# A transformer block pair on one core: first layer norm moved into the recurrence, stores awaited later, last tiles reordered

## Chip, cores, metric

One core of a Trainium2 chip. The metric is the device time of one launch in microseconds (us), the median of several runs. Engines are named as in the profile: PE is TensorE, DVE is VectorE, ACT is ScalarE, POOL is GpSimd, SP is SyncE, which issues all DMAs of this kernel.

## What is computed

Two blocks of the same outer form over x of 4 batches, 512 positions and 512 channels, in fp32. Of the reference only the outer form and the second block matter here:

```python
xn = layernorm(x)
x = x + attention0(xn) * silu(ffn0(xn))          # a recurrence over time, and a gated FFN
xn = layernorm(x)                                # of x1, as the kernel names it
# attention1: linear attention, 16 heads of 128, keys and values of 4 heads
q, k, v = xn @ Wq.T + bq, xn @ Wk.T + bk, xn @ Wv.T + bv
sq, sk = elu(q) + 1, elu(k) + 1
kv = einsum('bhsd,bhse->bhde', sk, v)
s = (sq @ kv) / (sum over d of sq * k_sum + 1e-6) @ Wo.T
# ffn1: relu between two products, weights of 4 bits with scales, plus a rank of 16
g = silu(relu(xn @ W_up + b_up + xn @ A_up @ B_up) @ W_dn + b_dn + relu(...) @ A_dn @ B_dn)
x = x + s * g
```

## The kernel before

Four stages follow each other, each a block of its own with a barrier of all engines at its end: `front` (norm and projections of attention 0), `recurrence_and_gate`, `linear_attention`, `relu_gate`. A batch is a tile of 128 partitions by 4 rows of 512 (TT = 4 tiles of 128 positions; KT = 4 tiles of 128 channels). The order of work is written out by hand for every engine; engines meet by semaphores. Products in full precision are made of three matmuls on split operands (`product3`, L701 to L703): a high part (rounded copy) and a low part (the rest). Buffers `relay[0..2]` (1 MB each) and `parts` outlive the stages and carry data over a barrier: loads for the next stage are issued before the barrier and counted by `handed`/`hand`.

`recurrence_and_gate`: VectorE's `unit` and GpSimd's `read` run the recurrence, TensorE the FFN. In the end of the last batch (`finish`, `silu`, then `attend` for t = 0 to 3) VectorE gates the attention's tiles, GpSimd's `add` adds them to x into `xs`, and SyncE stores each tile of x1 (L967) and waits until all have landed. Before that SyncE loads x1 of batch 0 into `relay[0]`, Wk into `relay[1]`, Wv into `relay[2]`.

`linear_attention`: the first batch needs `statistics`, `deviations` (GpSimd, a power), `normalise`, then TensorE's transposes (L2043), ScalarE's high parts `copy_x` (L1937), VectorE's low parts `low_x` (L1789). Beside it `high_kv` (L1928) and `low_kv` (L1702) split Wk and Wv. Then come products k and v of each batch, kv, and for 64 pairs of head and batch q, M and the heads; `accumulate` (L1852) sums the heads into `acc[b]`. At the end SyncE stores s of each batch and tile (L1691, 16 stores) and waits for all.

`relu_gate`: 16 steps a batch (UT = 16). Step j makes the up product of tile j; ReLU on ScalarE (L2425), the split of x2 on VectorE (L2377, L2379), and two steps later (LAG = 2) the down products for t = 0 to 3. In the first batch the weights of 4 bits are expanded beside it, two tiles a step: `expand` on VectorE (L2330, L2334), with a small product by `make` (L2452), `high` on ScalarE (L2397), the low part on GpSimd (L2297). A `make` of tile i waits for the expansion of tile i - 2. In the last steps the results of a batch are finished: z, tanh, gate on VectorE and ScalarE, and GpSimd adds to x1 in `xs` (two tiles), which SyncE loads and stores tile by tile.

## Time and profile before

| | |
|---|---|
| median of 3 runs | 1770.9 us (1768.85 to 1771.44) |
| profiled execution | 1772.48 us, its span 1770.7 us, mean granted clock 0.968 |
| PE busy | 1641.4 us (93%), 6704 matmuls |
| DVE busy | 1177.9 us (67%) |
| ACT busy | 394.4 us (22%) |
| POOL busy | 615.4 us (35%) |
| DMA | 200.45 MB, mean 113 GB/s |

```profile
PE   6899947999999999969999999999996899999996
DVE  6999755777878778746637777787875566242423
PEclk9999977999999999989999999999999899999998
DMA  5534457675676765513020000000003433101011
```

The four strips show the span in 40 equal slices of 44.3 us, each digit the busy share in tenths; PEclk is the granted clock of TensorE in tenths of full speed (2.4 GHz; 5 is 1.2 GHz). The recurrence ends in slice 18, the linear attention in slice 31, and `relu_gate` fills the rest. A busy PE is not PE at its peak: the ends of matmuls are modelled.

### The profile page before, as it was taken

To read this page: it belongs to the slowest core of one execution; us is meant where nothing else is said; L and a number is where in the kernel's file an instruction comes from. 1 tells how busy PE (TensorE), PEld (TensorE's weight loads), DVE (VectorE), ACT (ScalarE), POOL (GpSimd) and SP (SyncE) were. 2 spreads that over 40 slices of the span, in tenths; PEclk is the share of its full clock that TensorE was granted. 3 is DMA by queue.
4 is the path that set the end of the run, shared out by engine and by line. 5 is a ranking of instruction groups with operands and counts; after the bars stand their busy time and mean duration, and the time that the engine had idled before them with its cause. 6 is when DMAs were issued, how large, how long until landed. Compare 5 with 4: busy or idle time off the path is not lost. (4 is left out here: it accounts for less than half of the span.)

```text
span 1770.7 us, 20395 instructions
## 1 busy us (share of the span) xinstructions
PE 1641.4 (93%) x6704; PEld 1135.9 (64%) x6704; DVE 1177.9 (67%) x1694; ACT 394.4 (22%) x670; POOL 615.4 (35%) x455
## 2 busy tenths in 40 slices
PE   6899947999999999969999999999996899999996
PEld 3344425647646656528877777777774667888885
DVE  6999755777878778746637777787875566242423
ACT  1222220011021110112223333333332222121211
POOL 4586522445554565450003222232421242010101
PEclk9999977999999999989999999999999899999998
DMA  5534457675676765513020000000003433101011
GB/s 196 194 123 170 180 173 238 227 213 200 202 224 206 232 200 196 179 39 116 24 91 29 18 24 14 25 18 19 19 3 141 126 104 101 64 30 65 30 41 36
DMA packets 87329, 200.45 MB, mean 113 GB/s; under 512 B 7248, under 2 KB 29520, under 8 KB 79440
## 3 DMA queue, kind: packets, MB, share of 16 engines
q1 hardware_dynamic: 87248, 199.42, 33.9%
q8 instruction: 44, 0.72, 0.2%
q14 instruction: 37, 0.30, 0.1%
HBM read 156.41 MB, written 42.99 MB: 113 GB/s over the span
## 5 line engine op out<-in xcount | busy, mean ns | idle before, releaser
L986 POOL TENSOR_TENSOR r_rS<-r_S,r_rT 128x512 f32<-128x512 f32 x128 | 184.6, 1444 | 206.2 <-DVE r_S L1079 204.0
L1852 DVE SCALAR_TENSOR_TENSOR l_acc<-l_ps,l_inv,l_acc 128x512 f32<-128x512 f32 x240 | 167.3, 749 | 10.1 <-PE l_ps L703 10.1
L1079 DVE TENSOR_TENSOR_SCAN r_S<-r_dT,r_ps 128x512 f32<-128x512 f32 x128 | 156.4, 1222 | 17.3 <-POOL r_rS L986 13.2
L2377 DVE CAST g_x_part<-g_x 128x512 fp32r<-128x512 f32 x64 | 36.8, 574 | 188.6 <-ACT g_x L2425 188.6
L1430 PE MATMUL r_ps<-Wdn,r_h 128*128 128x512 f32 x352 | 154.6, 595 | 0.0
L1725 POOL TENSOR_TENSOR relay<-l_expq,l_reluq 128x512 f32<-128x512 f32 x42 | 54.4, 1295 | 190.7 <-ACT l_expq L2004 190.7
L1430 PEld LDWEIGHTS r_ps<-Wdn,r_h 128*128 128x128 f32 x352 | 65.7, 190 | 85.5 <-issue 85.4
L2304 POOL TENSOR_TENSOR g_xs<-g_xs,relay 128x512 f32<-128x512 f32 x16 | 21.4, 1336 | 262.3 <-DVE relay L2355 250.8
L1828 DVE TENSOR_SCALAR l_expq<-l_ps,l_bq 128x512 f32<-128x512 f32 x64 | 48.0, 750 | 89.0 <-ACT l_reluq L2000 86.9
L701 PE MATMUL l_ps<-l_M_part,l_sq_part 128*128 128x512 f32 x256 | 101.6, 397 | 3.9 <-DVE l_acc L1852 3.1
L701 PE MATMUL g_ps<-g_Wdn,g_x_part 128*128 128x512 f32 x256 | 103.7, 405 | 0.0
L701 PE MATMUL r_ps<-relay_part,r_w_part 128*128 128x512 f32 x224 | 94.4, 422 | 10.0 <-DVE r_h L1090 7.2
L702 PE MATMUL g_ps<-g_Wdn,g_x_part 128*128 128x512 f32 x256 | 101.2, 395 | 0.0
L703 PE MATMUL g_ps<-g_Wdn,g_x_part 128*128 128x512 f32 x256 | 101.2, 395 | 0.0
L703 PE MATMUL l_ps<-l_M_part,l_sq_part 128*128 128x512 f32 x256 | 100.7, 393 | 0.0
L702 PE MATMUL l_ps<-l_M_part,l_sq_part 128*128 128x512 f32 x256 | 100.3, 392 | 0.0
L703 PE MATMUL r_ps<-relay_part,r_w_part 128*128 128x512 f32 x224 | 91.2, 407 | 0.0
L702 PE MATMUL r_ps<-relay_part,r_w_part 128*128 128x512 f32 x224 | 91.1, 407 | 0.0
L2425 ACT ACTIVATE g_x<-g_ps,g_b_up 128x512 f32<-128x512 f32 x64 | 43.8, 685 | 205.7 <-PE g_ps L703 205.7
L2000 ACT ACTIVATE l_reluq<-l_ps,l_bq 128x512 f32<-128x512 f32 x64 | 44.1, 689 | 199.2 <-PE l_ps L703 199.1
L1285 ACT ACTIVATE r_tanh_gate<-r_ps 128x512 f32<-128x512 f32 x44 | 26.3, 597 | 274.7 <-PE r_ps L703 274.7
L701 PE MATMUL r_ps<-relay_part,first_part 128*128 128x512 f32 x128 | 55.4, 433 | 26.8 <-DVE relay_part L1059 22.4
(278 smaller groups left out, 3921.2 us busy)
## 6 DMA issues: line engine op xcount, KB each, us to landing
r_w_part<-scratch_wgu SPq DMA_DIRECT2D x28, 1024.0 KB, 7.0
r_V<-scratch_v SPq DMA_DIRECT2D x96, 256.0 KB
first_part<-scratch_wgu SPq DMA_DIRECT2D x16, 1024.0 KB, 5.4
relay<-scratch_x SPq DMA_DIRECT2D x11, 1024.0 KB, 6.7
scratch_wgu<-f_halves SPq DMA_DIRECT2D x28, 384.0 KB, 4.4
relay<-scratch_v SPq DMA_DIRECT2D x32, 256.0 KB
relay<-in_x SPq DMA_DIRECT2D x4, 1024.0 KB, 8.2
scratch_x<-f_xT SPq DMA_DIRECT2D x4, 1024.0 KB
```

The source lines that it names most:

```text
L701: nc.tensor.matmul(out, left[1], right[0], start=start, stop=False)
L702: nc.tensor.matmul(out, left[0], right[1], start=False, stop=False)
L703: return nc.tensor.matmul(out, left[0], right[0], start=False, stop=stop)
L986: nc.gpsimd.tensor_tensor(rS[u % RS][:, :], S[u % 2][:, 0:T], rT[u // DK][:, :], ALU.mult).then_inc(rS_ready.sem, 1)
L1079: nc.vector.tensor_tensor_scan(S[u % 2][:, 1:T + 1], dT[hh][:, :], kv, 0.0, ALU.mult, ALU.add).then_inc(S_ready.sem, 1)
L1430: last = nc.tensor.matmul(place[0][:, :], h[:, j, n * P:(n + 1) * P], Wdn[:, j, :], start=(j == 0), stop=(j == JT - 1))
L1725: nc.gpsimd.tensor_tensor(sq[i % N_SQ], expq[i % 2][:, :], reluq[i % 2][:, :], ALU.add).then_inc(sq_ready, 1)
L1828: nc.vector.tensor_scalar(expq[i % 2][:, :], place("q", i)[:, :], bq[:, h:h + 1], 0.0, ALU.add, ALU.min).then_inc(minq_ready, 1)
L1852: last = nc.vector.scalar_tensor_tensor(acc[b][:, t, :], ps, scale, acc[b][:, t, :], ALU.mult, ALU.add)
L2000: nc.scalar.activation(reluq[i % 2][:, :], place("q", i)[:, :], ACT.Relu, bias=bq[:, h:h + 1]).then_inc(reluq_ready, 1)
L2377: nc.vector.tensor_copy(hi[:, :], x2[j % 2][:, :]).then_inc(x2_hi_ready.sem, 1)
L2425: nc.scalar.activation(x2[j % 2][:, :], U.place(("up", j))[:, :], ACT.Relu, bias=b_up[:, j:j + 1]).then_inc(x2_ready.sem, 1)
```

## The change

In the recurrence's end VectorE makes the whole layer norm of batch 0 (`next_normalised`) between the last `silu` and the `attend`s, with the power on GpSimd, in place in `relay[0]`. The last of the four additions of x1 goes from GpSimd to VectorE. The stores of x1's last batch count on `x1_late`, which the stage doesn't await; the linear attention awaits it on SyncE before the load of batch 3 and on VectorE before the key operations. There the statistics and the normalisation of batch 0 are gone, the low parts 0 and 1 of Wk are made by VectorE, and ScalarE copies x between the splits of Wk and Wv.

At the end of the linear attention s goes out in four stores, one a batch, counted on `s_late` and awaited by SyncE in `relu_gate` ahead of the first load of s. There ScalarE's first ReLU waits for b_up alone, and in step 0 ReLU and split come before the expansions. The last batch of TensorE is written out behind the loop; its last 12 down products run tiles 0 and 1 first, then tile 2, then tile 3 (`END`). x1 is loaded whole into `relay[1]` (4 tiles), and the words of W_dn have a buffer of their own.

```diff
@@ recurrence_and_gate, SyncE
             sp.wait_ge(*F.product(("gu", JT - 1), B - 1))
-            sp.dma_start(relay[0][:, :, :], rows(x1, 0)).then_inc(hand, 16)
+            sp.dma_start(relay[0][:, :, :], rows(x1, 0)).then_inc(next_x_loaded, 16)
...
             for t in range(TT):
-                sp.wait_ge(*x1_ready.now(B, t + 1))
-                sp.dma_start(x1[(B - 1) * T + t * P:(B - 1) * T + (t + 1) * P, :], xs[:, t, :]).then_inc(
-                    x1_stored.sem, 16)
-            sp.wait_ge(x1_stored.sem, 16 * (B + TT))
+                if t < TT - 1:
+                    sp.wait_ge(*x1_ready.now(B, t + 1))
+                else:
+                    sp.wait_ge(last_x1_ready, 1)
+                sp.dma_start(x1[(B - 1) * T + t * P:(B - 1) * T + (t + 1) * P, :], xs[:, t, :]).then_inc(x1_late, 16)
+            sp.wait_ge(x1_stored.sem, 16 * B)
@@ GpSimd
             body(B - 1, False, True)
-            for t in range(TT):
+            pool.wait_ge(next_step, 3)
+            nc.gpsimd.tensor_tensor(next_rstd[:, :], next_veps[:, :], half[:, 0:TT], ALU.pow).then_inc(next_step, 1)
+            for t in range(TT - 1):
                 add(B, t)
@@ VectorE
+            def next_normalised():
+                dve.wait_ge(next_x_loaded, 16)
+                for t in range(TT):
+                    last = nc.vector.bn_stats(next_stats[:, t, :], relay[0][:, t, :])
+                last.then_inc(next_step, 1)
...
+                for t in range(TT):
+                    last = nc.vector.bn_aggr(next_mv[:, t, :], next_stats[:, t, :])
+                last.then_inc(next_step, 1)
+                dve.wait_ge(next_step, 2)
+                nc.vector.tensor_scalar(next_veps[:, :], next_mv[:, :, 1], 1e-5, None, ALU.add).then_inc(next_step, 1)
+                dve.wait_ge(next_step, 4)
+                for t in range(TT):
+                    nc.vector.tensor_scalar(relay[0][:, t, :], relay[0][:, t, :], next_mv[:, t, 0:1], next_rstd[:, t:t + 1],
+                                            ALU.subtract, ALU.mult)
...
                 silu(b, 3)
+                next_normalised()
                 for t in range(TT):
                     attend(b + 1, t, F.place(("s", 0)) if t < 2 else O)
+                dve.wait_ge(*x_loaded.before(b + 1, 1))
+                dve.wait_ge(*sg_ready.now(b + 1, TT))
+                nc.vector.tensor_tensor(xs[:, TT - 1, :], xs[:, TT - 1, :], u1[TT - 1], ALU.add).then_inc(last_x1_ready, 1)
@@ linear_attention, SyncE
-            sp.wait_ge(handed, 3 * 16)
...
             sp.wait_ge(*product("xT", 1, KT - 1))
+            sp.wait_ge(x1_late, TT * 16)
             load_x(3)
...
             for b in range(B):
-                for t in range(TT):
-                    sp.wait_ge(acc_ready, ((QH - 1) * B + b) * TT + t + 1)
-                    sp.dma_start(slab(spill["s"], b)[:, t * C:(t + 1) * C], acc[b][:, t, :]).then_inc(s_stored, 16)
-            sp.wait_ge(s_stored, 16 * B * TT)
+                sp.wait_ge(acc_ready, ((QH - 1) * B + b + 1) * TT)
+                sp.dma_start(slab(spill["s"], b), flat(acc[b][:, :, :])).then_inc(s_late, 16)
@@ GpSimd
-            low_kv("k", 0)
-            low_kv("k", 1)
-            deviations(0)
+            pool.sem_inc(rstd_ready, 1)
             low_kv("k", 2)
             low_kv("k", 3)
@@ VectorE
-            statistics(0)
-            normalise(0)
+            for s in (stats_ready, mv_ready, var_ready):
+                dve.sem_inc(s, 1)
+            dve.sem_inc(xn_ready, TT)
+            for kt in range(2):
+                dve.wait_ge(wkv_hi_ready["k"], kt + 1)
+                nc.vector.tensor_tensor(Wkv["k"][1][:, kt, :], raw["k"][:, kt, :], Wkv["k"][0][:, kt, :].bitcast(F32),
+                                        ALU.subtract).then_inc(wkv_lo_ready["k"], 1)
             low_x(0)
+            dve.wait_ge(x1_late, TT * 16)
@@ ScalarE
-            act.wait_ge(handed, 3 * 16)
+            act.wait_ge(handed, 2 * 16)
             high_kv("k")
+            copy_x(0)
             high_kv("v")
-            copy_x(0)
@@ relu_gate
+    END = [(t, i) for i in range(UT - 1 - LAG, UT) for t in range(2)]
+    END += [(t, i) for t in range(2, TT) for i in range(UT - 1 - LAG, UT)]
...
-        xs = sb("xs", [P, 2, C])
-        up_q, dn_q = s[:, :, :].bitcast(I32), xs[:, :, :].bitcast(I32)
+        xs = relay[1]
+        dn_words = sb("dn_words", [P, 2, C], I32)
@@ SyncE
-                load(0)
-                load(1)
+                sp.wait_ge(*out_stored.before(b, TT))
+                sp.dma_start(xs[:, :, :], rows(x1, b)).then_inc(x1_loaded.sem, 16)
                 for t in range(TT):
                     sp.wait_ge(*out_ready.now(b, t + 1))
-                    sp.dma_start(out[bass.ds(b * T + t * P, P), :], xs[:, t % 2, :]).then_inc(out_stored[t % 2].sem, 16)
-                    if t + 2 < TT:
-                        load(t + 2)
+                    sp.dma_start(out[bass.ds(b * T + t * P, P), :], xs[:, t, :]).then_inc(out_stored.sem, 16)
...
             sp.wait_ge(expanded, 2 * len(order))
+            sp.wait_ge(s_late, 16 * B)
             finish(0)
@@ VectorE (ScalarE likewise with high(x))
-                    if first:
+                    if first and j > 0:
                         for x in tiles_at(j):
                             expand(x)
...
                     nc.vector.tensor_tensor(lo[:, :], x2[j % 2][:, :], hi[:, :].bitcast(F32), ALU.subtract).then_inc(
                         x2_lo_ready.sem, 1)
+                    if first and j == 0:
+                        for x in tiles_at(j):
+                            expand(x)
@@ ScalarE
-                    act.wait_ge(small_loaded, 2 * 16)
+                    act.wait_ge(b_up_loaded, 16)
@@ TensorE
+                    if last_batch and n == UT - 1:
+                        for t, i in END:
+                            pe.wait_ge(*x2_lo_ready.now(b, i + 1))
+                            product = down(b, t, i)
+                            if i == UT - 1:
+                                product.then_inc(Y.done.sem, 1)
+                        return
...
-            with pe.Fori(1, B) as b:
+            with pe.Fori(1, B - 1) as b:
                 sequence(b, False)
+            sequence(B - 1, False, True)
```

## Rows read from the trace of the kernel before

**Rows 1.** Stretches: us, busy (instructions) of each engine, PEclk, DMA share, GB/s.
```profile
800.50:930.00 129.50, 128.53 (x674) 104.77 (x672) 68.52 (x128) 33.48 (x64) 8.77 (x8) 1.00 0.22 73
1373.60:1402.34 28.74, 25.56 (x81) 17.32 (x81) 16.16 (x22) 6.88 (x12) 9.36 (x8) 0.81 0.42 114
...
1430.90:1459.86 28.96, 27.47 (x104) 18.79 (x105) 17.37 (x24) 7.43 (x13) 10.44 (x9) 1.00 0.37 109
...
1500.00:1757.00 257.00, 256.36 (x1110) 208.10 (x1108) 80.82 (x131) 41.02 (x63) 12.84 (x10) 1.00 0.12 42
```
**Rows 2.** Order of time, PE: start, us, line, out<-in, count [idle before <-releaser].
```profile
793.64 0.45 PE L2043 MATMUL l_ps<-ident,relay 128*128 128x128 f32 x1 [11.89 <-DVE relay L1783]
...
800.45 0.53 PE L701 MATMUL l_ps<-l_Wk,kept_x_part 128*128 128x512 f32 x1
```
**Rows 3.** Chain that ended last, start of the stage relu_gate: start, us, what.
```profile
1373.22 0.34 SPq L2255
...
1378.24 5.18 DMA g_b_dn<-in_b_dn
```
**Rows 4.** The same chain, at the end of the span.
```profile
1754.47 0.70 DVE kept_scale L2347
...
1766.92 1.28 POOLq L2130
```
**Rows 5.** Line L967, SyncE's stores of x1: ns min/median/max of the issue.
```profile
L967 SPq DMA_DIRECT2D scratch_x<-r_xs x4: 332/338/349, 780.5 to 785.1; - x4
...
DMA to landing us min/median/max: 2.0/2.0/2.0
```
**Rows 6.** Order of time, DVE, from the recurrence's end on.
```profile
778.36 1.41 DVE L1165 SCALAR_TENSOR_TENSOR r_u<-r_ps,r_hyr,r_u 128x512 f32<-128x512 f32 x2 [5.76 <-PE r_ps L1358]
781.79 1.41 DVE L1165 SCALAR_TENSOR_TENSOR r_u<-r_ps,r_hyr,r_u 128x512 f32<-128x512 f32 x2 [2.02 <-PE r_ps L1358]
787.59 2.47 DVE L1769 BATCH_NORM_STATS2 l_stats<-relay 128x6 f32<-128x512 f32 x4 [4.39 <-PEq L753]
...
792.02 5.69 DVE L1783 TENSOR_SCALAR relay<-relay,l_mv,l_rstd 128x512 f32<-128x512 f32 x4 [1.14 <-POOL l_rstd L1707]
...
818.37 1.92 DVE L1783 TENSOR_SCALAR relay<-relay,l_mv,l_rstd 128x512 f32<-128x512 f32 x4 [1.13 <-POOL l_rstd L1707]
```
**Rows 7.** Order of time, ACT (first row) and POOL.
```profile
787.58 2.19 ACT L1928 ACTIVATE l_Wk<-relay 128x512 fp32r<-128x512 f32 x4 [14.73 <-PEq L753]
...
782.62 2.48 POOL L999 TENSOR_TENSOR r_xs<-r_xs,r_u 128x512 f32<-128x512 f32 x2 [0.88 <-DVE r_u L1165]
...
788.36 2.50 POOL L1702 TENSOR_TENSOR l_Wk<-relay,l_Wk 128x512 fp32r<-128x512 f32 x2 [0.64 <-ACT l_Wk L1928]
```
**Rows 8.** Stretches of one us at the stage's start, for PEclk (third from the end).
```profile
787.00:788.00 1.00, 0.00 (x0) 0.00 (x0) 0.41 (x1) 0.42 (x1) 0.16 (x2) 0.50 0.00 0
...
800.00:801.00 1.00, 1.00 (x6) 0.96 (x5) 0.84 (x2) 0.80 (x2) 0.07 (x1) 0.72 0.07 16
```
**Rows 9.** Line L1691, SyncE's stores of s: ns min/median/max of the issue.
```profile
L1691 SPq DMA_DIRECT2D scratch_s<-l_acc x16: 424/709/1062, 1355.6 to 1367.0; - x16
...
DMA to landing us min/median/max: 5.4/6.5/6.9
```
**Rows 10.** Stretches for DMA: the last two columns are its share and GB/s.
```profile
1360.00:1365.00 5.00, 1.87 (x9) 1.21 (x7) 2.66 (x4) 0.00 (x0) 0.00 (x0) 1.00 1.05 396
...
1375.00:1380.00 5.00, 5.00 (x17) 3.55 (x17) 1.04 (x2) 0.00 (x0) 0.00 (x0) 0.76 0.78 229
```
**Rows 11.** Order of time in the expansion, DVE (first row) and PE.
```profile
1387.34 0.68 DVE L2330 SCALAR_TENSOR_TENSOR g_whole<-relay,g_z 128x512 f32<-128x512 int32 x1
...
1385.22 0.80 PE L701 MATMUL g_ps<-kept_x_part,kept_up 128*128 128x512 f32 x1 [1.92 <-ACT g_x L2425]
1385.81 0.63 PE L702 MATMUL g_ps<-kept_x_part,kept_up 128*128 128x512 f32 x1
1386.24 0.63 PE L703 MATMUL g_ps<-kept_x_part,kept_up 128*128 128x512 f32 x1
```
**Rows 12.** Order of time, DVE, its last instruction.
```profile
1763.15 0.69 DVE L2355 SCALAR_TENSOR_TENSOR relay<-relay,g_z 128x512 f32<-128x512 f32 x1
```

More of the change, by code:

```diff
@@ L1457, in _, with linear_attention @@
                 counted = F.index[job] + 1
-def linear_attention(nc, w, x1, spill, relay, parts, ident, kept, handed, hand):
+def linear_attention(nc, w, x1, spill, relay, parts, ident, kept, handed, x1_late, hand, s_late):
     UNITS = QH * B
@@ L2107, in _, with relu_gate @@
                 last.then_inc(done, 1)
-def relu_gate(nc, w, x1, spill, out, relay, parts, kept, handed):
+def relu_gate(nc, w, x1, spill, out, relay, parts, kept, handed, s_late):
     LAG = 2
@@ L2426, in sequence @@
                                          bias=b_up[:, j:j + 1]).then_inc(x2_ready.sem, 1)
+                    if first and j == 0:
+                        for x in tiles_at(j):
+                            high(x)
             act.sem_inc(w_hi_ready, len(first_tiles))
@@ L2591, in build, with stages @@
         handed = [outer.enter_context(nc.semaphore(f"handed{i}")) for i in range(3)]
-        stages(nc, w, out, spill, x1, relay, parts, ident, handed)
-def stages(nc, w, out, spill, x1, relay, parts, ident, handed):
+        x1_late = outer.enter_context(nc.semaphore("x1_late"))
+        s_late = outer.enter_context(nc.semaphore("s_late"))
+        stages(nc, w, out, spill, x1, relay, parts, ident, handed, x1_late, s_late)
+def stages(nc, w, out, spill, x1, relay, parts, ident, handed, x1_late, s_late):
     with ExitStack() as ctx:
@@ L2614, in stages @@
         kept["narrow"] = sb("narrow", [P, C])
[L2615 to L2616 removed]
+        linear_attention(nc, w, x1, spill, relay, parts, ident, kept, handed[1], x1_late, handed[2], s_late)
+        relu_gate(nc, w, x1, spill, out, relay, parts, kept, handed[2], s_late)
 def kernel(**inputs):
```

65 lines of the change are left out of this document (33 added, 32 removed).

## The prediction

> **What bounds the kernel now.** I read the stages first (busy time by stretch), then the waits and the order of time at the three places where the stretches leave holes. [rows 1]: in the first 129.5 us of the linear attention TensorE is busy 128.5 us, and in the last 257 us before the end 256.4 us. These stretches are bound by TensorE: what is won ahead of them arrives at the end whole. In the expansion of the weights (from 1373.6) it is busy 25.6 of 28.7 us at a mean clock of 0.81, later 27.5 of 29.0: there the expansion by VectorE, ScalarE and GpSimd leads, and TensorE has about 1.5 us of slack in each 29. Three holes remain.
> Hole A: TensorE is done with the recurrence at 781.8, starts its transposes at 793.64 after 11.89 us idle, and the first key product at 800.45 [rows 2].
> Hole B: the last accumulation ends at 1362.66, and SyncE's first instruction of the next stage is at 1373.22 [rows 3]. The expansion then starts slowly.
> Hole C: the last product ends about 1756.4, the span at 1770.7 [rows 4].
>
> **Part A, norm and stores.** Before: the last store of x1 is issued at 785.1 and lands 2.0 us later [rows 5], and the end barrier comes after it; then statistics, GpSimd's power and normalisation (787.59 to 797.71), transposes, copies.
> The norm is moved into VectorE's idle time of 5.76 us ahead of 778.36 [rows 6]. Its price there: from the start of the statistics to the power's result 4.43 us (787.59 to 792.02), and four normalisations at 0.48 us as in the row of 818.37, where GpSimd rests, not 1.42 us as at 792.02, where it works [rows 6]. That is 4.43 + 1.92 = 6.35 us, 0.6 us more than the gap. The first two gatings slip by that; the last two wait for a product that ends at 781.8 and don't move. So the norm costs nothing on the path (bounds: 0, and 0.6 if all slips). Its power is queued on GpSimd behind the last inverse and ahead of the additions; GpSimd is idle there. Its load of relay[0] is far ahead.
> The last addition goes from GpSimd (ends 785.10 [rows 7]) to VectorE, behind the last gating at 783.20. VectorE takes 0.69 us for such an operation alone; beside GpSimd's third addition (to about 783.9) it waits at most for that one. I take 784.5. SyncE issues the last store in 0.35 us and no longer waits for its landing; the barrier took 0.4 us after the landing. New start of the stage: 785.4 instead of 787.55, won 2.15 us (bounds 1.6 and 2.7). Three small loads queue on SyncE behind the stores; their reader comes 6 us later.
> In the new stage ScalarE splits Wk first (2.19 us for four [rows 7]), then copies x, then splits Wv. Low parts 0 and 1 of Wk are VectorE's, 2 and 3 GpSimd's: the third high part is there at 1.7 us, two GpSimd operations of 1.25 us [rows 7] end at 4.2. Beside it, transposes 0.3 to 4.0 even at the low clock, copies from 2.2 on, VectorE's low x from 2.9 to 5.7. TensorE's key product starts at 4.4 us of the stage instead of 12.9 (800.45 less 787.55), 8.5 us sooner. GpSimd has the low parts of Wv at about 10.8, their use is at about 16. The wait for x1_late stands on VectorE ahead of the key operations, at about 6 us of the stage; the stores (2 us) have long landed. On SyncE it stands before the load of batch 3.
> TensorE's clock: the granted clock was at 0.50 from 787 and rose within 800 to 801 [rows 8], after 2.7 us of dense transposes; so the old products started nearly at 2.4 GHz. Now only some 2 us of transposes stand ahead of them, behind 4 us of rest. If 3 us of products lie at 1.2 GHz, half is lost, 1.5 us; bounds 0 and 1.7. I take 1.5, since the nearest stretch, the transposes from 793.64 to 800, lay wholly at the low level. Sum A: 2.15 + 8.5 - 1.5 = **9.1 us** (7.3 to 11.2). Behind it TensorE is the bound [rows 1], so it stays.
> VectorE's two low parts of Wk have two operands in SBUF, and GpSimd works beside the second. [rows 6] show 1.42 against 0.48 us with and without GpSimd. The Trainium skill (GPSIMD Engine Reference, Specifications) says that the SBUF interfaces are shared with VectorE, in two-port modes or with two SBUF inputs. By that the second low part would wait for one GpSimd operation, and the low x would start some 0.3 us later. The sum can do without it.
>
> **Part B, s and the expansion.** Before: 16 stores of 256 KB, issued from 1355.6 to 1367.0 at 709 ns each, landing 5.4 to 6.9 us after issue [rows 9], and SyncE waits for the last. I read that as a backlog: the DMA engines are full at 396 GB/s in 1360 to 1365 [rows 10].
> Now: four stores of 1 MB, the last issued at 1362.7, not awaited. Issue 0.4 to 0.6 us, barrier 0.5: start of the stage about 1363.8 instead of 1373.22, 9.4 us sooner. But the 5.24 MB (s, and 1 MB of up_q issued at 1355.05) are not fewer: at 400 GB/s from about 1356.9 they end at 1370.0. All loads of the new stage are queued behind: b_up lands at about 1370.5 instead of 2.2 us after issue; up_scale, dn_q and the first dn_scale are 1.0 MB, 3.5 us at the 290 GB/s that this mix would give (229 at a share of 0.78 [rows 10]), so dn_scale lands at 1374.3.
> This rests on order in the queue, for which the landing times grown to 6.9 us speak. The Trainium skill (DMA: Bandwidth & Descriptors, Queues, rings and completion order) says that on each engine descriptors are consumed in ring order; by that, the trace agrees, small loads don't overtake the stores, which speaks against part of this change's gain.
> Then: the first product needs 5.1 us at 1.2 GHz (twelve matmuls 0.43 us apart, as 1385.81 and 1386.24 [rows 11]) and is done at about 1369.5. ScalarE waits only for b_up, so its first ReLU (before: after two weight splits that waited for b_dn, which landed at 1383.42 [rows 3]) is at 1370.6. VectorE splits x2 to 1372.6, expands its first tile to 1374.0, the second 1374.3 to 1375.7 (its scale); GpSimd's low part of the first ends at 1376.0, so the third tile starts at 1376.1. Before it started at 1387.34 [rows 11]: **11.2 us** sooner. From there the same instructions follow in the same order, with the same loads of up_q.
> TensorE: its third up product waits for the second tile's expansion, because a small product is queued ahead of it: 1376.2, against 1385.22 [rows 11], 9.0 us sooner and, as before, at the low clock. It is 2.2 us behind the expansion's gain, and has slack of 1.5 us in each stretch: used up by the second, so the 11.2 stay. Bounds: 6.6 (below, SyncE held) and 14.
> The bigger SBUF buffers and the split semaphore for b_dn cost nothing: b_dn is first used in the next batch.
>
> **Part C, end.** TensorE does the same last 12 products in another order, tiles 0 and 1 first; x2's last part is there at 1750.0 and now used at 1750.6, so it doesn't stall. Tile 0 is done 4 products earlier, 12 matmuls of 0.234 us, 2.8 us, tile 3 as before. VectorE's end chain starts at 1751.7 instead of 1754.47 and, with z of tile 3 at 1757.2 (product at 1756.4), ends at 1761.2 instead of 1763.84 [rows 12]. GpSimd's last addition no longer waits for a store and a load into the same buffer (the addition started at 1766.92 [rows 4]): it runs 1761.2 to 1762.5, and 2.5 us for the last store, as before, end at 1765.0. Won **5.7 us**. If the other order helped nothing, 3.1; bounds 3.1 and 6.0. x1 whole (1 MB) and s are loaded some 70 us earlier; SyncE loses its waits between them. The last batch written out behind the loop costs code to fetch; the loop's turns before show no gap [rows 1]. Bounds 0 and 1 us, I take 0.
>
> **Sum.** 9.1 + 11.2 + 5.7 = 26.0 us. The profiled execution took 1772.5 us (span 1770.7); it would take 1746.5. It lies 1.6 above the median of 1770.9, so the median would be **1744.9**.
>
> **Rivals.**
> (1) The forecast as above, 1741 to 1748: chance 0.50.
> (2) No backlog for the new loads, and the clock up sooner in A: B gives 13 to 14 (then TensorE's own work binds), A 10.5: about 1741, down to 1738. For it: 8 KB of b_up could pass; against it: the stores' landing times. By the Trainium skill's rule of ring order this case doesn't come. 0.17.
> (3) SyncE is held: 709 ns an issue against 338 for stores of x1 [rows 5, 9] says that it is throttled when much is queued. Four stores of 1 MB may block it until the queue has room, in the worst case to 1370. Then the first product ends at 1375.1, ReLU, split and two tiles take 5.6 us, the third tile starts at 1380.7, B gives 6.6 and the total is 21.4: 1749.5. 0.23.
> (4) A or B yields still less (later loads of weights, low clock in both, 17 to 20 us won): 1751 to 1754. 0.06.
> (5) Slower than before: TensorE stays at 1.2 GHz through much of the expansion, because its products come in shorter pieces between the new waits. Each us of product there costs 0.5 us. To eat 26 us, some 52 us of the 86 must lie at the low level beyond today's 11; from 60 us on the kernel is slower by over 0.2%. All 75 more would cost 37 and give 1782. Against it: in the stretch from 1430.9 it stood at 1.00 with the same rhythm [rows 1]. 0.02.
> (6) It does not do what it says: SyncE's end of the stage still comes only when all stores have drained, in A and in B, and the loads come behind it: little more than C is left, near 1762 to 1767. 0.02.
>
> **How the numbers follow.** The likeliest case gives 1744.9. For 8 in 10 the range takes in (1), (2) and (3) nearly whole: 1738 to 1752. What a measurement of this kernel can tell is about 0.2%, 3.5 us. Faster by more 0.96, within 0.02, slower 0.02.
>
> **What would show it.** A: no VectorE statistics at the stage's start, last gating still near 783.2, key product 4.4 us behind the first load of biases; if 6 or more, Wk's low parts are late. The clock row of the first 4 us of products tells 1.5 from 0. B: the issue of the last store of s near 1362.7; if next-stage loads are issued after 1367, it is (3); the landing time of b_up, 6 us or 2, tells (1) from (2); third tile's start relative to 1376.1 (shifted by A). C: span's end 8.6 us behind the last product instead of 14.3. It would be wrong if TensorE, at the low clock, were the last thing in the expansion's stretches.

## The result, and the profile after

| | before | changed |
|---|---|---|
| first timing, median | 1771.17 us (4 runs) | 1755.53 us (1749.87 to 1757.08, 4 runs) |
| ratio, 95% interval | | 0.9905 (0.9882 to 0.9928) |
| second timing, ratio | | 0.9884 (0.986 to 0.9909) |
| third timing, ratio | | 0.9886 (0.9862 to 0.9911) |
| profiled execution, span | 1772.48, 1770.7 us | 1749.87, 1748.1 us |

The change won 15.6 us by the first timing; the mean of the three ratios is 0.9892, or 19.1 us. The forecast was 26.0 us and 1744.9: the direction was right, the size too large, and the 1755.5 lies above the upper end of the range, 1752.

PE, DVE and the granted clock of the changed kernel in 40 slices of its span:

```profile
PE   6899846899999999989999999999998899999997
DVE  6999855777877879756637777787777466242423
PEclk9999977999999999999999999999999899999999
```

The strips are nearly those of before: the gain lies in three places that are shorter than a slice of 44 us. So I compare landmarks instead, instructions that every variant has. The work before the first landmark, the start of the last s-projection of the recurrence, ends anywhere from 770.3 to 775.0 in 17 profiles, whichever the kernel: that is scatter and belongs to no part.

| profile | s-proj. to first key product | to last accumulation | to last product | to end of span | third tile |
|---|---|---|---|---|---|
| before | 27.50 | 562.21 | 393.70 | 14.34 | 24.7 |
| changed | 16.35 | 563.71 | 387.01 | 9.46 | 18.2 |
| changed, second profile | 16.69 | 565.55 | 385.99 | 9.49 | 17.7 |
| changed, third profile | 16.34 | 563.80 | 388.54 | 9.49 | 19.0 |

Each column is the time from the landmark to its left, in us; the last one is the start of the third expanded tile behind the last accumulation (before: 1387.34 [rows 11] less 1362.66). The first column is A, the second the clock's share of it, the third B, the fourth C. The s-projection takes 7.1 us in some profiles and 8.8 in others, with part of it at 1.2 GHz, so A has to be read between profiles alike in that: without A the first two columns sum to 588.0 to 588.2 (three profiles, 7.1) and 589.7 (before, 8.8); with A to 580.1 (four) and 581.9 to 582.2 (four). Run 11 below, also without A, has 592.6: the same code lost 2.9 us more to the low clock there. The means of all profiles, 589.3 in the five without A and 581.1 in the eight with A and no fillers, differ by 8.2. **A is worth 7.6 to 8.2 us by the profiles.** B's column is 392.3 to 393.7 in the four profiles without B, mean 393.1, and 386.0 to 388.5 in the five that have all three parts with B's code as the change has it, mean 387.3: **B is worth 5.8 us** (3.8 to 7.7 between single profiles; 5.6 if run 3, B alone at 388.8, is counted in). **C is worth 4.85.** Together 18.4 to 18.9, beside 19.1 by the timings.

What B did is seen in SyncE's rows of the changed kernel and in the last accumulation's (start, us, engine, line):

```profile
1348.84 2.79 DVE L1877 SCALAR_TENSOR_TENSOR l_acc<-l_ps,l_inv,l_acc 128x512 f32<-128x512 f32 x4 [1.07 <-PE l_ps L703]
...
1344.05 0.55 SPq L1718 DMA_DIRECT2D relay<-in_up_q  x1
1344.65 7.34 SPq L1722 DMA_DIRECT2D scratch_s<-l_acc  x4
1352.66 0.34 SPq L2282 DMA_DIRECT2D g_b_up<-in_b_up  x1
```

The last accumulation ends at 1351.63, and the stage's first load is issued 1.03 us behind it; before it was 10.56 (1362.66 to 1373.22 in [rows 3]). The views of these two lines (ns min/median/max of the issue, then time to landing):

```profile
L1722 SPq DMA_DIRECT2D scratch_s<-l_acc x4: 332/378/611, 1344.6 to 1351.7; - x4
DMA to landing us min/median/max: 9.0/10.2/11.8
...
DMA to landing us min/median/max: 8.9/8.9/8.9
```

A store of s is issued in 378 ns instead of 709 [rows 9]: SyncE is not held. But a store of 1 MB lands after 10.2 us, and the 8 KB of b_up, the last line, after 8.9. Why, the stretches of the changed kernel show (last two columns: share and GB/s of the DMA engines):

```profile
1345.00:1350.00 5.00, 3.51 (x16) 2.61 (x15) 3.93 (x7) 0.00 (x0) 0.00 (x0) 1.00 0.89 227
1350.00:1355.00 5.00, 2.61 (x10) 1.85 (x9) 1.63 (x3) 0.00 (x0) 0.00 (x0) 0.91 1.02 428
1355.00:1360.00 5.00, 5.00 (x17) 3.46 (x17) 0.00 (x0) 0.00 (x0) 0.00 (x0) 0.75 1.00 411
1360.00:1365.00 5.00, 1.22 (x6) 0.66 (x4) 1.12 (x2) 0.69 (x1) 0.00 (x0) 0.93 1.03 229
```

The stores go at 411 to 428 GB/s, as reckoned. The load of up_q ahead of them moves only 227 GB/s at a share of 0.89, the first packets of the stores included, and the loads of scales and of the first words of W_dn behind them 229 at 1.03. ScalarE and VectorE wait for what stands at the end of that queue:

```profile
1361.54 0.69 ACT L2454 ACTIVATE g_x<-g_ps,g_b_up 128x512 f32<-128x512 f32 x1 [18.28 <-DMA g_b_up<-in_b_up]
...
1366.09 0.69 DVE L2356 SCALAR_TENSOR_TENSOR g_whole<-relay,g_z 128x512 f32<-128x512 int32 x1 [2.67 <-DMA g_z<-in_up_scale]
...
1367.93 0.69 DVE L2356 SCALAR_TENSOR_TENSOR g_whole<-g_dn_words,g_tanh_z 128x512 f32<-128x512 int32 x1 [0.43 <-DMA g_tanh_z<-in_dn_scale]
...
1369.88 0.69 DVE L2356 SCALAR_TENSOR_TENSOR g_whole<-relay,g_z 128x512 f32<-128x512 int32 x1 [0.54 <-POOL g_Wup L2324]
```

These are the first ReLU and the expansions of the first three tiles: 9.9, 14.5, 16.3 and 18.2 us behind the last accumulation. The forecast had 7.9, 9.9, 11.6 and 13.4.

### The profile page after: what moved, and what is told of

It reads as the page before. It is cut to its first block and busy times, and to the rows that moved or that the text cites. A ratio compares the mean times of both kernels' runs of the same rounds, so it can differ in the third digit from the quotient of the medians.

```text
span 1748.1 us, 20338 instructions
## 1 busy us (share of the span) xinstructions
PE 1635.2 (94%) x6704; PEld 1132.9 (65%) x6704; DVE 1179.0 (67%) x1697; ACT 394.1 (23%) x670; POOL 612.9 (35%) x452
## 5 line engine op out<-in xcount | busy, mean ns | idle before, releaser
L2331 POOL TENSOR_TENSOR relay<-relay 128x512 f32<-128x512 f32 x16 | 21.7, 1355 | 257.1 <-DVE relay L2381 257.1
L701 PE MATMUL r_ps<-relay_part,r_w_part 128*128 128x512 f32 x224 | 92.9, 415 | 10.9 <-DVE r_h L1102 8.1
L702 PE MATMUL r_ps<-relay_part,r_w_part 128*128 128x512 f32 x224 | 89.6, 400 | 0.0
L703 PE MATMUL r_ps<-relay_part,r_w_part 128*128 128x512 f32 x224 | 89.5, 400 | 0.0
```

What stands on the lines that cost most here:

```text
L701: nc.tensor.matmul(out, left[1], right[0], start=start, stop=False)
L702: nc.tensor.matmul(out, left[0], right[1], start=False, stop=False)
L703: return nc.tensor.matmul(out, left[0], right[0], start=False, stop=stop)
```

## The experiments

All timings stand beside runs of the kernel before on the same chip: runs 1 to 4 together, then 5 to 8, 9 to 12, 13 to 15. "Third tile", "last product" and the like are counted behind the last accumulation, as in the table above.

**Run 1, the changed kernel again.**

> The changed kernel as it is, timed beside its parts. The theory (backlog in B, and a clock that falls or not at short waits of TensorE): 14 to 22 us won over the kernel before, with single runs 5 us or more apart, since its four runs lay between 1749.9 and 1757.1. In the trace, counted from the end of the last accumulation: the third expanded tile starts 18.3 us later. The rival (the first trace was a lucky run, the loss lies in a stage that was not looked at): some stretch other than the stage starts differs from the first trace by more than 3 us.

Measured: 1752.06 us, ratio 0.9884 (0.986 to 0.9909), span 1750.5; its landmarks stand above. The third tile starts at 17.7 (expected 18.3), and the gain is nearer to 20 us than to the first timing's 15.6.

**Runs 2 to 4, each part alone** (the other parts' lines as in the kernel before):

```diff
@@ A alone: norm in the recurrence, x1_late
+                next_normalised()
@@ B alone: unawaited stores, early ReLU
+                sp.dma_start(slab(spill["s"], b), flat(acc[b][:, :, :])).then_inc(s_late, 16)
@@ C alone: order of the end, x1 whole
+                        for t, i in END:
+                sp.dma_start(xs[:, :, :], rows(x1, b)).then_inc(x1_loaded.sem, 16)
```

> Part A alone (norm of the first batch in the recurrence's end, stores of x1 not awaited, Wk's low parts shared, x copied ahead of Wv). Theory from the two traces: 11.1 us won, less a dip of the clock in the linear attention now and then (1.5 us): 9.5 to 11. My blind sum had 9.1. Rival: A wins its 11 us at its own place, but less arrives at the end (under 7), because the linear attention or the expansion gives it back.

Measured: 1761.97, ratio 0.9937 (0.9914 to 0.996). s-projection to last accumulation 582.06 (before 589.71), the rest as before. That is 7.65 us, while the ratio of the timing says 11 (7 to 15); the profile is of one of the slower executions of run 2. So theory and rival, 9.5 to 11 us or under 7, are not clearly told apart; 7.65 lies between them.

> Part B alone (s in four stores not awaited, ReLU ahead of the expansion in step 0, b_up on its own semaphore). Theory: 6 to 7 us won, since the loads of the stage come behind the stores of s: from the last accumulation to the third tile 18 to 18.5 us instead of 24.7. The blind sum had 11.2. Rival: B is worth 11 alone and only the combination with A loses.

Measured: 1766.9, ratio 0.9968 (0.9952 to 0.9985). Last accumulation to last product 388.84 instead of 393.1, third tile at 18.0. B falls short alone too, so the rival is out. The landmarks give 4.3 us, less than the expected 6 to 7, which the timing (5.7, 2.7 to 8.5) leaves open.

> Part C alone (last products in another order, x1 whole in a buffer of four tiles). Theory: the span's end 9.4 us behind the last product instead of 14.3, 4.9 us won; blind 5.7. Rival: the batch written out behind the loop, or the 1 MB load, costs in the last batches: under 3 us won, and the stretch between the expansion's end and the last product is longer than before's 296.5 us.

Measured: 1766.49, ratio 0.9976 (0.9957 to 0.9994). Last product to end 9.47 instead of 14.34, the other columns as before: the expected 4.9 us.

The three parts stand in three separate columns, with 7.65, 4.3 and 4.9 us alone: 16.9, against 18.4 in the whole, within the scatter of B's column. So nothing shows that the forecast's gain was lost between the parts; by the landmarks each was sized too large by itself, B most.

**Run 5, a quarter of s stored.** This kernel leaves out three quarters of s, in the stores and in the later loads.

```diff
-                sp.dma_start(slab(spill["s"], b), flat(acc[b][:, :, :])).then_inc(s_late, 16)
+                sp.dma_start(slab(spill["s"], b)[:, 0:C], acc[b][:, 0, :]).then_inc(s_late, 16)
...
-                sp.dma_start(flat(s[:, :, :]), slab(spill["s"], b)).then_inc(s_loaded.sem, 16)
+                sp.dma_start(s[:, 0, :], slab(spill["s"], b)[:, 0:C]).then_inc(s_loaded.sem, 16)
```

> The changed kernel, but each of the four stores of s writes only its first quarter (256 KB of 1 MB), and the load of s in the last stage reads only that quarter; three quarters of s are left out. Theory 1 (backlog): the loads of the next stage were late only because 4 MB of stores lay ahead of them. Then b_up lands 2 to 4 us behind its issue instead of 8.9, up_scale before the first ReLU is through, and the third expanded tile starts at most 14 us behind the last accumulation instead of 18.2: 4 to 6 us sooner than in the changed kernel, some 5 us less in the whole. Theory 2 (the loads are slow by themselves: broadcast scales, bytes of up_q): b_up lands sooner, the scales do not, and the third tile starts 17 to 18 us behind, within 1 us of the changed kernel. Theory 3 (the gain is eaten by TensorE's clock in the expansion): the third tile starts sooner, but the tile behind the next load of up_q stays 41 to 43 us behind the last accumulation.

Measured: 1745.69 us, ratio 0.9846 (0.9828 to 0.9863). b_up lands after 2.6 us, and the first ReLU waits for TensorE and no longer for a DMA:

```profile
1357.08 0.69 ACT L2454 ACTIVATE g_x<-g_ps,g_b_up 128x512 f32<-128x512 f32 x1 [14.65 <-PE g_ps L703]
```

It is 6.3 us behind the last accumulation, the third tile 12.8, the last product 383.3. Theory 1 holds: the bytes of the stores account for 4.0 us (387.3 less 383.3) of the 5.4 that B lacked. The step from there to the last product takes 370.5 us, against 369.0 before and 368.8 in the changed kernel, so 1.5 to 1.8 us are left for theory 3.

**Run 6, the stores issued by ScalarE's queue.**

```diff
+                act.wait_ge(acc_ready, ((QH - 1) * B + b + 1) * TT)
+                act.dma_start(slab(spill["s"], b), flat(acc[b][:, :, :])).then_inc(s_late, 16)
@@ relu_gate, ScalarE, ahead of the first expanded tile's high part
+                    act.wait_ge(s_late, 16 * B)
```

> The changed kernel, but the four stores of s are issued by ScalarE's queue at the end of its program instead of SyncE's; ScalarE waits for their landing ahead of the high part of the first expanded tile. Theory 1 (order within a queue): the next stage's loads on SyncE's queue do not stand behind the stores any more; they only share the engines' bandwidth with them. b_up lands in 3 to 5 us instead of 8.9, and the third tile starts 14 to 16 us behind the last accumulation instead of 18.2: 2 to 4 us less in the whole than the changed kernel. Theory 2 (the bytes are the limit, not the order): 5 MB must go through anyway, the scales land as late as before, and the time stays within 1 us of the changed kernel's. ScalarE's wait could cost up to 1 us if the stores land later than 13 us behind the last accumulation.

Measured: 1750.11, ratio 0.9878 (0.986 to 0.9896). The scales come sooner, the first tile starts at 10.9 us instead of 14.5, the third at 15.6 instead of 18.2, as theory 1 had it; but the last product is at 385.9, the time of theory 2, beside 386.0 to 388.5 in the changed kernel. No store stands ahead of b_up in its queue any more, and still it lands 8.0 us after issue, against 8.9. What does stand ahead of it there is the load of up_q. Time to landing of up_q (first line) and b_up:

```profile
DMA to landing us min/median/max: 12.6/12.6/12.6
...
DMA to landing us min/median/max: 8.0/8.0/8.0
```

The load of up_q took 12.6 us here and 7.1 in the changed kernel. It was issued at 1342.84 and landed at 1355.4, 3.9 us behind the issue of b_up; b_up landed at 1359.5, just behind the last store (1359.3). What held up_q, the DMA queues show from 1346 to 1354 (q10 is ScalarE's, q1 SyncE's; packets, MB, share of the 16 DMA engines):

```profile
q10 hardware_dynamic: 358, 2.67, 79.0%
q1 hardware_dynamic: 361, 0.74, 23.9%
```

The two queues took turns packet by packet, and a store's packet held 8 KB where one of up_q held 2 KB. The Trainium skill (DMA: Bandwidth & Descriptors, Queues, rings and completion order) says that an engine serves its queues in turn, packet by packet; the trace agrees. So the order in the queue, the forecast's reason, held b_up behind up_q, and the stores held both from another queue, by their turns. How a small load fares with nothing ahead of it in its own queue was not tried.

**Run 7, TensorE kept busy in two pauses of the linear attention.** The fillers are products whose results are overwritten.

```diff
+FILL_K, FILL_Q = 7, 8
...
+                            for _ in range(FILL_K):
+                                nc.tensor.transpose(out[:, 0:P], ident[:, :], ident[:, :])
                         pe.wait_ge(wkv_lo_ready[kind], KT)
@@ ahead of the first product with the second head's Wq
+                                for _ in range(FILL_Q):
+                                    nc.tensor.matmul(out[:, :], x_part[b][0][:, 0, 0:P], x_part[b][0][:, 0, :],
+                                                     start=True, stop=True)
```

> The changed kernel, with two fillers on TensorE in the linear attention, whose results are overwritten: seven 128x128 transposes of the identity between the transposes of batch 0 and the first key product, and eight 128x512 products ahead of the first product with the second head's Wq, where TensorE waited 2.1 us. Theory 1 (the clock takes part of A): without the pauses the granted clock stays or rises, the first key products are 0.23 us apart instead of 0.43, and the dip behind the 2.1 us wait goes; from first key product to last accumulation 562.5 us as in the kernel before, instead of 563.7 to 565.5; 1 to 3 us less in the whole. Theory 2 (the clock does not hang on these pauses): the stretch stays at 563.7 to 565.5, and the fillers cost up to 0.5 us.

Measured: 1750.75, ratio 0.9875 (0.9858 to 0.9891). First key product to last accumulation 562.29: theory 1. The gain of 1.4 to 3.3 us in this stretch is clear in the traces and too small for these timings.

**Run 8, the changed kernel without the early ReLU.**

```diff
-                    if first and j > 0:
+                    if first:
                         for x in tiles_at(j):
                             expand(x)
```

> The changed kernel with one edit of part B undone: the first ReLU and split again follow the expansion of the first two tiles, and ScalarE waits for b_up and b_dn together. The forecast counted on the early ReLU and split (they were to run while the scales are awaited). Theory 1 (scales late, backlog): the first tile waits for up_scale to about 14 us behind the last accumulation whatever the order is, so moving ReLU and split behind the tiles puts 2 to 3 us of work back on the path: the third tile starts 20 to 21 us behind instead of 18.2, and the whole takes 1.5 to 3 us more. Theory 2 (the order does nothing, all of B is the stores): within 0.5 us of the changed kernel.

Measured: 1758.04, ratio 0.9914 (0.9896 to 0.9933). Third tile at 21.2, last product at 389.7: 2.4 us behind the mean of the changed kernel. Theory 1: while the scales are awaited, ReLU and split are free.

**Run 9, two stores ahead of up_q.** SyncE waited for the load of up_q until 1344.05, while the first two sums had been ready at 1338.3 and 1342.7 and the DMA engines rested.

```diff
+            for b in range(2):
+                sp.wait_ge(acc_ready, ((QH - 1) * B + b + 1) * TT)
+                sp.dma_start(slab(spill["s"], b), flat(acc[b][:, :, :])).then_inc(s_late, 16)
             sp.wait_ge(*sq_split(UNITS - 1))
             sp.wait_ge(*product("rows", QH - 1))
             sp.dma_start(relay[0][:, :, :].bitcast(I32),
...
-            for b in range(B):
+            for b in range(2, B):
```

> The changed kernel, with the stores of s of batches 0 and 1 issued ahead of the load of up_q that SyncE issues last but one in the linear attention. Their sums are ready at 1338.3 and 1342.7 in the changed kernel's trace, but SyncE stood until 1344.05 at the wait for that load and issued all of them behind it; the DMA engines rested before. Theory 1 (backlog of bytes): 2 MB are gone by then, b_up lands 3 to 6 us behind its issue instead of 8.9, the third tile starts 13 to 15.5 us behind the last accumulation instead of 18.2, and the whole takes 2 to 4 us less than the changed kernel, nearly as little as with a quarter of s stored. Theory 2 (what delays the loads is not bytes but the broadcast scale loads, or TensorE's clock eats the gain): the third tile starts sooner, the whole takes within 1 us of the changed kernel's time.

Measured: 1749.9, ratio 0.9862 (0.9842 to 0.9881). Stores and b_up of this kernel, time to landing, in this order: the first two stores, the last two, b_up.

```profile
DMA to landing us min/median/max: 3.9/4.0/4.2
...
DMA to landing us min/median/max: 4.4/5.4/6.4
...
DMA to landing us min/median/max: 3.6/3.6/3.6
```

Third tile at 12.6, last product at 381.5, where the forecast had thought the changed kernel (393.7 less 11.2). All of s is stored. Theory 1.

**Run 10, the stores of run 9, the two fillers of run 7, and nine more fillers at the attention's end.** Beside run 9, the last of these:

```diff
+            pe.wait_ge(*reader[jobs[len(jobs) - len(banks)]])
+            for _ in range(FILL_END):
+                nc.tensor.matmul(banks[len(jobs) % len(banks)][:, :], x_part[0][0][:, 0, 0:P], x_part[0][0][:, 0, :],
+                                 start=True, stop=True)
```

> The kernel with the stores before up_q, and with three fillers on TensorE, whose results are overwritten: the two of the run before (ahead of the first key product, and ahead of the first product with the second head's Wq), and nine 128x512 products behind the last product of the linear attention, in the 2.4 us in which TensorE waits for the next stage. Theory 1 (the clock hangs on the pauses): from the end of the s-projection to the last accumulation 570.3 us as in the run with the two fillers (573.0 in the changed kernel), and the first product of the last stage takes 2.8 us instead of 4.6 from first to last matmul, which counts if b_up has landed by then; 3 to 5 us less in the whole than the stores before up_q alone. Theory 2 (the two gains overlap: the last stage is held by the loads, not by the product): only the 2.7 us of the two fillers.

Measured: 1746.78, ratio 0.9842 (0.9826 to 0.9859). s-projection to last accumulation 579.2; last product at 383.5. The first product of the last stage is through sooner, but b_up was issued 1.8 us behind the last accumulation instead of 1.0, and the first tile waits 1.09 us for its scale. Theory 2 on the last stage: what held it was the loads, not the first product.

**Run 11, the order of the end alone.** Of part C only `END`; x1 in quarters as before.

```diff
+                        for t, i in END:
+                            pe.wait_ge(*x2_lo_ready.now(b, i + 1))
+                            product = down(b, t, i)
```

> The kernel before with one half of part C: in the last batch the products with Wdn go in the new order, tiles 0 and 1 first; x1 is still loaded in quarters into two buffers. Theory 1 (the forecast's split: 2.6 us from the order, 3.1 us from the whole load of x1): the span ends 11.7 us behind the last product instead of 14.3. Theory 2 (the halves overlap: with tiles 0 and 1 done sooner, their stores and the loads into their buffers are done sooner as well, so GpSimd's last addition does not wait any more): it ends 9.5 to 10 us behind, as with both halves, and the whole load of x1 is worth nothing here.

Measured: ratio 0.9991 (0.9978 to 1.0003), span 1771.4. The timing can't tell it from the kernel before. This profile's attention lost 2.9 us more to the low clock (565.1 us from first key product to last accumulation, against 562.2), which hides in the span what the end won. Its code there is that of the kernel before, and still the clock was low at the first key products and fell behind the wait of 2.1 us (products 0.43 us apart, as at 1.2 GHz):

```profile
935.39 0.77 PE L701 MATMUL l_ps<-kept_x_part,l_Wq_part 128*128 128x512 f32 x1 [2.10 <-POOL l_Wq_part L1711]
935.95 0.63 PE L702 MATMUL l_ps<-kept_x_part,l_Wq_part 128*128 128x512 f32 x1
936.38 0.63 PE L703 MATMUL l_ps<-kept_x_part,l_Wq_part 128*128 128x512 f32 x1
```

Last product to end 11.5 us instead of 14.3: theory 1. The order is worth 2.8 us (forecast 2.6), the whole load 2.0 (forecast 3.1). Why the second half fell short, VectorE's last row shows here (first) and in the changed kernel:

```profile
1763.90 0.69 DVE L2356 SCALAR_TENSOR_TENSOR relay<-relay,g_z 128x512 f32<-128x512 f32 x1
```

```profile
1742.66 1.63 DVE L2381 SCALAR_TENSOR_TENSOR relay<-relay,g_z 128x512 f32<-128x512 f32 x1
...
1742.10 1.64 POOL L2331 TENSOR_TENSOR relay<-relay 128x512 f32<-128x512 f32 x1 [1.35 <-DVE relay L2381]
```

With x1 there in whole, GpSimd's third addition runs beside VectorE's last gate, and both take longer: 1.63 instead of 0.69. That gate ends at 1744.29, 0.55 us behind the addition, which had started first. In run 11 a load holds GpSimd's third addition until 1764.23, when that gate is half through; there the gate takes 0.69 and the addition 1.49 us instead of 1.26. Before it was 0.69 as well [rows 12]. The Trainium skill (GPSIMD Engine Reference, Specifications) says that the two engines share SBUF interfaces, with contention for VectorE's instructions of two SBUF inputs; this trace agrees.

**Run 12, the stores of s alone** (the stores and their late wait, the first step in its old order).

```diff
+                sp.wait_ge(acc_ready, ((QH - 1) * B + b + 1) * TT)
+                sp.dma_start(slab(spill["s"], b), flat(acc[b][:, :, :])).then_inc(s_late, 16)
```

> The kernel before with one half of part B: four stores of s that the stage does not wait for; first ReLU and split behind the first two tiles as before, b_up and b_dn awaited together. Theory 1 (the halves add up, as the changed kernel without the early ReLU says): the first load of the last stage 1.0 us behind the last accumulation instead of 10.6, the third tile 21.2 us behind it instead of 24.7, last product 389.7 to 390.5 us behind it instead of 393.7, so 3.2 to 4 us less in the whole. Theory 2 (the stores alone are worth nothing, since ScalarE waits for b_dn at the end of a backlog): the third tile 23.5 us behind or later, under 1.5 us in the whole.

Measured: 1771.34, ratio 0.9986 (0.9972 to 1.0001). Third tile at 21.6, last product at 390.6, 2.5 us less than without B: nearer to theory 1, just past its weak end. So 9.4 us at the stage's start became 2.5 at its end.

**Runs 13 to 15.** The changed kernel; the stores of run 9 with the two fillers of run 7; the changed kernel with the first filler alone.

> The changed kernel unaltered, beside the two below. By the traces' sum (A 7.5 to 8.0, B 6.7 to 7.7, C 4.9) it takes 19 to 20.6 us less than the kernel before, a ratio of 0.989; if the first timing was right and the traces flatter it, 0.9905 or more.

> The stores of s of batches 0 and 1 before the load of up_q, and the two fillers of the linear attention, without the nine at its end. Theory 1 (the gains add: 573.3 to 570.3 us from the s-projection to the last accumulation by the fillers, 386.5 to 381.5 from there to the last product by the stores; the end fillers cost 2 us, since SyncE's first load came 0.75 us later and the scales with it): 7 to 8 us less than the changed kernel, 1.5 to 2 less than with the end fillers as well. Theory 2 (the 381.5 of that one profile was chance of the clock): 383 to 384 again, 5 to 6 us less than the changed kernel.

> The changed kernel with the seven transposes ahead of the first key product alone. Theory 1 (two losses of about 1.5 us each, one at the first products, one behind the 2.1 us wait at 919): from first key product to last accumulation 563.7 us instead of 565.5 (both) and 562.3 (none), and the dip behind the wait stays. Theory 2 (the dip is an echo of the low clock at the start): with the first products at full clock the dip is gone too, 562.3.

Measured: 1753.42, 1746.66 and 1754.53 us; ratios 0.9886 (0.9862 to 0.9911), 0.9854 (0.983 to 0.9879) and 0.9896 (0.9869 to 0.9922).

| run | key product to last accumulation | to last product | third tile |
|---|---|---|---|
| 13 | 563.80 | 388.54 | 19.0 |
| 14 | 562.28 | 384.27 | 13.3 |
| 15 | 562.42 | 387.39 | 18.4 |

Run 13's ratio is the expected 0.989, but its B column gives 4.6 us, not the expected 6.7 to 7.7. Run 14 is 6.8 us faster than run 13 beside it by the medians (the intervals of the ratios overlap a little), and 7.0 in the spans; with run 10 it is the second kernel that lies well below the changed one, at 1746.7 and 1746.8 us. Its second theory was the right one on the last stage: the 381.5 of run 9 did not come again. The three kernels with the stores ahead have 381.5, 384.3 and 383.5, mean 383.1, so that edit is worth 4.2 us beyond the change; the end fillers do nothing that can be told.

In run 15, with the first filler alone, both losses of clock are gone, though the wait of 2.1 us stays (one profile). Rows of TensorE's granted clock (third from the end) behind that wait, in the second profile of the changed kernel and in run 15:

```profile
920.00:925.00 5.00, 2.90 (x10) 1.97 (x9) 3.28 (x3) 1.93 (x4) 3.77 (x3) 0.80 0.32 102
925.00:930.00 5.00, 5.00 (x23) 3.15 (x22) 0.75 (x1) 1.75 (x4) 0.35 (x1) 0.86 0.02 4
```

```profile
920.00:925.00 5.00, 4.28 (x23) 2.90 (x23) 3.18 (x4) 1.32 (x2) 1.86 (x2) 1.00 0.19 54
925.00:930.00 5.00, 5.00 (x28) 3.97 (x25) 2.89 (x6) 2.33 (x5) 1.30 (x1) 1.00 0.02 5
```

Its timing shows no gain; 1 to 3 us are below what these intervals can tell. The stretch has 562.3 to 562.5 us in the four kernels with a first filler and 563.7 to 565.6 in the eight others with part A. Theory 2 has the number, but its reason fails: in the changed kernel's first profile the first key products ran at 2.4 GHz (0.23 us apart), and the dip came all the same. Without A it is 562.2 to 562.4 in four profiles and 565.1 in run 11, so these losses don't come with A alone, and that run 15's single profile has no dip may be chance.

## Why the prediction was wrong

**A: 9.1 forecast, 7.6 to 8.2 measured by the profiles; the timing of A alone, 7 to 15 us, leaves both open.** The key product started 4.39 us behind the stage's start in the changed kernel (forecast 4.4), held by the low part of Wk on GpSimd as the forecast said. The stage's start failed in part. With the s-projection at 8.8 us it came 2.3 us sooner (forecast 2.15). With the s-projection at 7.1 us the norm was no longer hidden:

```profile
775.35 1.92 DVE L1194 TENSOR_SCALAR relay<-relay,r_next_mv,r_next_rstd 128x512 f32<-128x512 f32 x4 [1.13 <-POOL r_next_rstd L1052]
777.18 2.94 DVE L1177 SCALAR_TENSOR_TENSOR r_u<-r_ps,r_hyr,r_u 128x512 f32<-128x512 f32 x4
780.22 0.89 DVE L1220 TENSOR_TENSOR r_xs<-r_xs,r_u 128x512 f32<-128x512 f32 x1
```

The four gatings run back to back behind the normalisation, and the last product, done at 778.68, waits for VectorE: only 0.95 us is won. "The last two wait for a product" held for the s-projection of 8.8 us that [rows 6] go with, not for the one of 7.1. The clock's term was put at 1.5 us with bounds 0 and 1.7, for the first products alone. Measured are 1.5 in the profiles with the short s-projection and 3.3 with the long: the first products at 1.2 GHz, as forecast, cost 1.8 there (3.3 less 1.5),

```profile
790.91 0.63 PE L701 MATMUL l_ps<-l_Wk,kept_x_part 128*128 128x512 f32 x1
791.34 0.63 PE L702 MATMUL l_ps<-l_Wk,kept_x_part 128*128 128x512 f32 x1
```

and in all of them a dip behind the wait at 919 costs some 1.5, of which the profile before has none behind the same wait. That second term was missing from the sum. But run 11 shows both losses, 2.9 us, in the code of before: over all profiles A costs 1.8 us of clock (means 564.6 and 562.9), so the 1.5 that was put in was nearly right on the average. The lower bound of A does not follow from its terms: 1.6 and 8.5 less 1.7 and 0.6 make 7.8, not 7.3.

**B: 11.2 forecast, 5.8 measured.** This is the step that put the result outside the range: the price of the loads behind the stores. The start of the stage was right (9.5 us sooner, forecast 9.4), and so was the claim that later steps keep the gain (from the third tile to the last product 368.3 to 369.8 us in those five profiles, 370.9 in run 3, before 369.0). The backlog itself was forecast, and sized too small twice. First, "at 400 GB/s from about 1356.9" priced the 1 MB of up_q like a store. The trace of before had its rate, in a stretch that the forecast left out:

```profile
1357.00:1359.00 2.00, 0.51 (x3) 0.14 (x2) 1.79 (x3) 0.00 (x0) 0.00 (x0) 1.00 0.82 184
```

That stretch holds up_q alone, and the first stretch of [rows 10], on which the forecast's 400 rested, held stores. At some 200 GB/s up_q needs 5 us instead of 2.6, and b_up landed 9.9 us behind the last accumulation instead of 7.8. Second, the scales and the first words of W_dn were priced at 290 GB/s and 3.5 us; they went at 229 and less. The first tile waited 2.67 us for its scale, where the forecast had no wait, and the second tile's scale landed at 1367.84, 16.2 us behind the last accumulation instead of 11.6. Run 5 (fewer bytes) and run 9 (the same bytes earlier) bring the third tile to 12.8 and 12.6 us, where the forecast had it at 13.4. Run 6 shows that it isn't the order in SyncE's queue alone: stores on another queue hold the loads too, by their turns.

**C: 5.7 forecast, 4.85 measured.** The order gave 2.8 (forecast 2.6). The end behind the last gate took what was reckoned, but that gate took 1.63 us instead of 0.69, beside GpSimd's third addition. The forecast had weighed that very slowing in A and not in C, where the engines now overlap.

**The rivals.** (3) named 1749.5, and the third tile's 18.2 us match its 18.0, but by another way: SyncE was not held, the loads were slow. (2), no backlog, is what run 5 shows, 1745.7 rather than 1741. (4), 1751 to 1754, held the second and third timing and had only 0.06: I had treated the three terms' errors as if they would cancel, while each term was read at its favourable end (hidden norm, one clock loss, full DMA rate, undisturbed gate), so they added: up to 1.3, 5.4 and 0.85, together 7.6 us.

## What to carry to other kernels

Taking a wait on stores away moves its cost to the loads behind it: price the bytes still in flight, each kind at its own rate from the trace, and look for idle DMA time ahead of the last accumulation in which part of them can go, as run 9 did. Stores on another queue still slow the loads (run 6). When engines are brought closer together, look up what each operation costs beside its new neighbour, and where work is hidden in a gap, ask how long the gap is in other executions. A sum of terms each taken from its good case needs a range that reaches to all bad cases at once.

## Unexpected in the hardware

A load of 1 MB took 12.6 us instead of 7.1 when 1 MB stores went on another queue: the two queues sent 361 and 358 packets in 8 us, of 2 KB and 8 KB, so the load moved 0.74 MB and the stores 2.67 (run 6). A two-input operation of VectorE took 1.63 us instead of 0.69 when GpSimd's addition had started before it, and 0.69 when the addition started second (run 11 and the kernel before).

With seven transposes of the identity between the real ones and the first key product the granted clock rose in the first us or so of the key products, and it stayed at 1.00 also behind a wait of 2.1 us some 130 us later (run 15, one profile). Behind that wait it fell in all eight profiles of part A without fillers, and of the five without A it fell in one (run 11). Why it falls in one execution and not in another of the same code was not found out.
